# A decoder layer on one core: plain fp32 products for the experts and the router, and the experts' SiLU from one activation

## The reference

```python
scores = softmax(xt @ gate_w.T)
top_vals, top_idx = lax.top_k(scores, 2)
combine = sum(one_hot(top_idx, 8) * top_vals[..., None], axis=1)
h = silu(xt @ W1 + B1) * (xt @ W3 + B3)          # for each expert
acc = acc + c[:, None] * (h @ W2 + B2)
z = silu(xt @ sw1 + sb1) * (xt @ sw3 + sb3) @ sw2 + sb2   # the shared one
```

## Time and profile before

| | us |
|---|---|
| median of three executions | 1228.98 (1221.31 to 1236.30) |
| span of the profiled execution, first to last instruction | 1224.7 |
| PE / PEld busy | 929.7 / 700.9 |
| DVE busy | 922.6 |
| ACT busy | 489.6 |
| POOL busy | 528.2 |

### The profile page before, as it was taken

One profiled execution on the slowest core, in us unless ns is written; L12 is line 12 of the kernel. 1 busy time (PEld: TensorE's weight loads), 2 busy tenths in 40 slices (PEclk: granted clock), 3 DMA queues, 4 the chain that ended last, 5 costly groups with the idle time before them and its releaser, 6 DMA issues.

```text
span 1224.7 us, 13783 instructions
## 1 busy us (share of the span) xinstructions
PE 929.7 (76%) x3960; PEld 700.9 (57%) x3960; DVE 922.6 (75%) x1323; ACT 489.6 (40%) x911; POOL 528.2 (43%) x311
## 2 busy tenths in 40 slices
PE   4845549668689899577689899486789896677996
PEld 2434435256468685165477785165468683554885
DVE  2699996589999966689999965789789965322233
ACT  3534423544246434454345424454245421211442
POOL 1266540453457740533367730544257741001553
PEclk9855558778669999678679899678579997665999
DMA  5100101201023211101023211201023212000331
GB/s 193 36 35 35 52 1 35 70 35 61 18 70 121 77 45 54 70 35 61 18 78 127 73 36 55 85 18 61 18 72 119 86 35 91 21 1 9 117 109 42
DMA packets 38254, 72.61 MB, mean 59 GB/s; under 512 B 3871, under 2 KB 12712, under 8 KB 38174
## 3 DMA queue, kind: packets, MB, share of 16 engines
q1 hardware_dynamic: 38174, 71.65, 17.8%
HBM read 65.14 MB, written 2.30 MB: 55 GB/s over the span
## 4 chain that ended last, share of the span: by engine, by line
PE 45%; DVE 23%; issue 20%; POOL 6%; ACT 3%; DVEq 1%; POOLq 0%; DMA 0%; ACTq 0%; SPq 0%
PE ps L862 11%; DVE hs L1051 7%; PE ps L939 7%; PE ps L718 6%; PE ps L797 5%; POOL dbu L531 4%; DVE yacc L1103 4%; PE ps L836 3%; PE ps L791 2%; PE ps L825 2%; DVE work L1219 2%; PE ps L881 2%; PE ps L776 2%; DVE xn L1014 1%; POOL work L563 1%
## 5 line engine op out<-in xcount | busy, mean ns | idle before, releaser
L531 POOL TENSOR_TENSOR dbu<-v,bbc 128x1024 f32<-128x1024 f32 x128 | 308.9, 2418 | 257.3 <-DVE hs L1051 136.3
L1051 DVE TENSOR_TENSOR_SCAN hs<-ps,carry,dbu 128x512 f32<-128x512 f32 x256 | 313.3, 1266 | 10.1 <-ACT ps L627 8.2
L627 ACT ACTIVATE ps<-delta,neg_a 128x512 f32<-128x512 f32 x256 | 175.7, 692 | 300.5 <-DVE hs L1051 300.4
L718 PE MATMUL ps<-ident,hs 128*128 128x128 f32 x1024 | 189.1, 344 | 116.5 <-DVE yacc L1103 99.5
L718 PEld LDWEIGHTS ps<-ident,hs 128*128 128x128 f32 x1024 | 157.0, 180 | 150.0 <-DVE hs L1051 72.4
L1103 DVE SCALAR_TENSOR_TENSOR yacc<-ps,ctok,yacc 128x512 f32<-128x512 f32 x240 | 167.3, 737 | 1.2 <-PE ps L718 1.0
L555 POOL TENSOR_TENSOR w_lo<-w13s,w_hi 128x512 fp32r<-128x512 f32 x72 | 94.5, 1313 | 145.1 <-ACT w_hi L693 145.1
L939 PE MATMUL ps<-w2s,work 128*128 128x256 f32 x576 | 140.4, 388 | 0.3
L939 PEld LDWEIGHTS ps<-w2s,work 128*128 128x128 f32 x576 | 109.0, 196 | 15.9 <-DVE work L1225 1.5
L1219 DVE SCALAR_TENSOR_TENSOR work<-work 128x512 f32<-128x512 f32 x72 | 82.3, 1143 | 46.5 <-POOL work L563 45.6
L862 PE MATMUL ps<-x_hi,w_hi 128*128 128x512 f32 x288 | 107.9, 457 | 9.4 <-DVE work L1225 9.2
(11 more groups left out here) (159 smaller groups left out, 1243.0 us busy)
## 6 DMA issues: line engine op xcount, KB each, us to landing
w13s<-in_w SPq DMA_DIRECT2D x72, 256.0 KB, 2.9
bbc<-brow_dram SPq DMA_DIRECT2D x32, 512.0 KB, 4.0
w2s<-in_w SPq DMA_DIRECT2D x36, 256.0 KB, 2.7
cbc<-comb_dram SPq DMA_DIRECT2D x32, 256.0 KB, 3.5
work<-work SPq DMA_DIRECT2D x16, 256.0 KB, 2.3
xn<-in_x SPq DMA_DIRECT2D x5, 512.0 KB, 5.3
xt<-in_x SPq DMA_DIRECT2D x4, 512.0 KB, 3.6
rope<-in_rope_q SPq DMA_DIRECT2D x4, 512.0 KB, 4.2
```

The lines of the kernel that those rows point to most:

```text
L531: pool.tensor_tensor(dbu[:, i % DRING, :, :], v[:, 2 * h:2 * h + 2, :], bbc[:, n // 2 % 2, n % 2, :].rearrange("p (o t) -> p o t", o=1) .t ...
L627: act.activation(ps[:, unit % 2, :], delta[:, q, :], ACT.Exp, scale=neg_a[:, q * NS + m:q * NS + m + 1]).then_inc(da_done.sem, 1)
L718: last = pe.transpose(ps[:, bank, t * P:(t + 1) * P], src(t), ident[:, :])
L1051: dve.tensor_tensor_scan(hs[:, m % 2, q, 0:TC], ps[:, unit % 2, :], dbu[:, n % DRING, q % 2, :], carry[:, m, q:q + 1], ALU.mult, ALU.add). ...
```

## The change

The gate products and the router's scores are formed in plain fp32 from the arrays as they are. The fp32r parts w13_hi, w13_lo, x2_hi, x2_lo and wgate_parts, and the instructions that write them, are gone; x2t, a plain copy of the transposed input, shares x1t's place. Each gate product is 2 plain products instead of 6 fp32r instructions. ScalarE writes SiLU(a + b1) with one activation, Silu; th and gm are gone, and VectorE writes hh from ga or gac at once. The ring w13s has 5 places instead of 3, and `load_half` waits for the W3 product that last read the place.

```diff
-HRING = 3
+HRING = 5
...
-        x2_hi = sb("x2_hi", [P, KD, TC])
-        x2_lo = sb("x2_lo", [P, KD, TC])
+        x2t = x1t
...
             def load_half(j, c):
-                if c >= HRING:
-                    sp.wait_ge(*lo_done.at(j, c - HRING + 1))
-                else:
-                    sp.wait_ge(*lo_done.at(j, 0))
+                sp.wait_ge(*b_ps.at(j, max(0, c - HRING + 1)))
...
-                c = t - T_EXP + 1 + HRING
+                c = t - T_EXP - 1 + HRING
                 if HRING <= c < 2 * ALL:
                     load_half(j, c)
...
-                    c = t - T_EXP + 1
-                    if 0 <= c < 2 * ALL:
-                        pool.wait_ge(*hi_done.at(j, c + 1))
-                        pool.tensor_tensor(w13_lo[:, c % HRING, :, :, :].bitcast(F32R), w13s[:, c % HRING, :, :, :],
-                                           w13_hi[:, c % HRING, :, :, :], ALU.subtract).then_inc(lo_done.sem, 1)
                     c = t - T_EXP - 1
                     if 2 <= c < 2 * ALL:
...
-                        pool.wait_ge(*gm_done.at(j, c - 1))
+                        pool.wait_ge(*hh_done.at(j, c - 1))
...
-                        act.activation(x2_hi[:, k, :].bitcast(F32R), ps[:, 4 + k, :], ACT.Copy).then_inc(x2hi_done.sem, 1)
-                c = t - T_EXP + 1
-                if 0 <= c < 2 * ALL:
-                    act.wait_ge(*w13_in[c % HRING].at(j, 16 * (c // HRING + 1)))
-                    act.wait_ge(*b_ps.at(j, max(0, c - HRING + 1)))
-                    act.activation(w13_hi[:, c % HRING, :, :, :].bitcast(F32R), w13s[:, c % HRING, :, :, :], ACT.Copy
-                                   ).then_inc(hi_done.sem, 1)
+                        act.activation(x2t[:, k, :], ps[:, 4 + k, :], ACT.Copy).then_inc(x2t_done.sem, 1)
...
                     act.wait_ge(*a_ps.at(j, c + 1))
-                    act.wait_ge(*gm_done.at(j, max(0, c - 1)))
-                    act.activation(ga[:, ib, :], ps[:, 4, :], ACT.Identity, scale=0.5, bias=bias
-                                   ).then_inc(ga_done.sem, 1)
-                    act.activation(th[:, ib, :], ps[:, 4, :], ACT.Tanh, scale=0.5, bias=bias
-                                   ).then_inc(th_done.sem, 1)
+                    act.wait_ge(*hh_done.at(j, max(0, c - 1)))
+                    act.activation(ga[:, ib, :], ps[:, 4, :], ACT.Silu, bias=col("b1", c)).then_inc(ga_done.sem, 1)
...
-                    pe.wait_ge(*lo_done.at(j, c + 1))
-                    pe.wait_ge(*th_done.at(j, c))
+                    pe.wait_ge(*w13_in[c % HRING].at(j, 16 * (c // HRING + 1)))
+                    pe.wait_ge(*ga_done.at(j, c))
                     gate_rows(j, c, 0, a_ps)
...
             def gate_rows(j, c, s, sig):
-                products(ps[:, 4 + s, :], lambda w, k: w[:, c % HRING, s, k, :], (w13_hi, w13_lo),
-                         lambda x, k: x[:, k, :], (x2_hi, x2_lo)).then_inc(sig.sem, 1)
...
+                for k in range(KD):
+                    last = pe.matmul(ps[:, 4 + s, :], w13s[:, c % HRING, s, k, :], x2t[:, k, :],
+                                     start=(k == 0), stop=(k == KD - 1))
+                last.then_inc(sig.sem, 1)
...
-                    pe.wait_ge(*x2lo_done.at(j, KD))
+                    pe.wait_ge(*x2t_done.at(j, KD))
                     for tile in range(NT):
...
+                        for k in range(KD):
+                            last = pe.matmul(ps[:, 6, tile * EXPERTS:(tile + 1) * EXPERTS],
+                                             x2t[:, k, tile * P:(tile + 1) * P], wgate[:, k, :],
+                                             start=(k == 0), stop=(k == KD - 1))
...
-                    dve.wait_ge(w_att.sem, 5 * 16)
-                    dve.tensor_copy(wgate_parts[:, :, 0:EXPERTS].bitcast(F32R), wgate[:, :, :]).then_inc(gate_split.sem, 1)
...
-                if t == T_GATE:
-                    for k in range(KD):
-                        dve.wait_ge(*x2hi_done.at(j, k + 1))
-                        dve.tensor_tensor(x2_lo[:, k, :].bitcast(F32R), ps[:, 4 + k, :], x2_hi[:, k, :], ALU.subtract
-                                          ).then_inc(x2lo_done.sem, 1)
...
-                    dve.wait_ge(*th_done.at(j, c + 1))
                     if c < 2:
                         dve.wait_ge(*ga_done.at(j, c + 1))
                     else:
                         dve.wait_ge(*gac_done.at(j, c - 1))
-                    dve.wait_ge(*hh_done.at(j, max(0, c - 1)))
-                    dve.scalar_tensor_tensor(out=gm[:, ib, :], in0=th[:, ib, :], scalar=1.0,
-                                             in1=(gac if c >= 2 else ga)[:, ib, :],
-                                             op0=ALU.add, op1=ALU.mult).then_inc(gm_done.sem, 1)
-                    dve.wait_ge(*gm_done.at(j, c + 1))
                     dve.wait_ge(*b_ps.at(j, c + 1))
                     dve.wait_ge(*o_ps.at(j, max(0, c - 1)))
                     dve.scalar_tensor_tensor(out=hh[:, ib, :], in0=ps[:, 5, :], scalar=col("b3", c),
-                                             in1=gm[:, ib, :], op0=ALU.add, op1=ALU.mult).then_inc(hh_done.sem, 1)
+                                             in1=(gac if c >= 2 else ga)[:, ib, :], op0=ALU.add, op1=ALU.mult
+                                             ).then_inc(hh_done.sem, 1)
...
-                dve.tensor_copy(lg_low[:, :, :], sums[:, :, 1, :]).then_inc(lg_low_done.sem, 1)
-                dve.wait_ge(*lg_low_done.at(j, 1))
-                dve.tensor_tensor(lg[:, :, :], sums[:, :, 0, :], lg_low[:, :, :], ALU.add).then_inc(lg_done.sem, 1)
+                dve.tensor_copy(lg[:, :, :], ps[:, 6, 0:NT * EXPERTS].rearrange("p (t e) -> p t e", t=NT)
+                                ).then_inc(lg_done.sem, 1)
```

44 lines of the change are left out of this document (5 added, 39 removed).

## The result

The changed kernel takes 1253.18 us (median of four executions, 1241.24 to 1257.10) against 1231.60 us for the kernel before on the same chip: ratio 1.0178, 95% interval 1.0105 to 1.0252. In a second comparison it took 1247.32 us, ratio 1.0149 (1.0084 to 1.0214). It is slower, by 1.5 to 1.8%. The forecast was 1255 us with 1237 to 1292, so the total came out as forecast. Its composition did not, and part of the agreement is luck; that is what the rest is about.

The account below looks back on a forecast made before the run. TensorE was taken to bound most steps, VectorE steps 6 to 10. Overlapped walks +13.3, last walk +13.4 and start -0.35 gave +26.4 us on the 1224.7 span, 1251.1; forecast median 1255 us, range 1237 to 1273.

Parts of the forecast that it names:

- TensorE's steps: Expert steps: plain gate products cost 0.5 to 0.7 us more per tick; 6.06 us beside a scan, 5.17 in last walk.
- Steps 6 to 10: VectorE's slow stretch in overlapped walks: losing four gm makes TensorE the bound, 30.47 to 25.3 us, -5.2 (-6.2 to 0).
- Table loads: ScalarE: 81 to 87 more loads of 1.28 us, each behind its wait, covered by TensorE's 6.06 us in overlapped ticks.
- +1.3 at each loop head: Head of each of three overlapped walks: the input's copy may get its own table load, 0 to 1.30 us, 1.30 taken.
- +1.3 for the attention's Exp: Last walk: the attention's Exp needs a table load, +1.3 us.
- +1.4 for the last walk's first Silu: Last walk: the first Silu needs a table load and step 1 waits for ga, +1.4 us.
- first rival: Overlapped ticks: table loads bind ScalarE; at 2.6 us a load, +45 us gives 1300 us; chance 0.16.
- third rival: ScalarE: one table serves both Silu and Exp, no load alternates, only 4 to 7 us go, 1249 us; chance 0.05.
- Steps 0 to 2: Router and first steps of an overlapped walk: earlier router start against first products at the low clock, together +0.3 us.
- second rival: Steps 0 to 2 of each walk: TensorE's 2.4 GHz clock granted two products earlier, 20 us in all, 1235 us; chance 0.10.
- Sum of the overlapped walks: Three overlapped walks: +7.7 - 5.2 + 0.3 + 0.35 + 1.3 = +4.4 us each, +13.3 in all.
- the forecast's own +4.3: Whole run: the median time lies 4.3 us above the span of the trace, added to get from span to forecast.

Follow-up runs that it names:

- eighth run: The changed kernel with four of the eight instructions of each gate product, summing only half of the rows; 1153.32 us in one execution.
- second run: The kernel before with split products kept, but SiLU as one Silu activation and no gm; 1217.08 us, ratio 0.9914 to the kernel before.
- first run: The changed kernel with plain products but the old SiLU back (ga, tanh and VectorE's gm); 1243.53 us, ratio 1.0127 to the kernel before.
- third run: The changed kernel with Tanh in Silu's place, so that no table load alternates; 1247.93 us, ratio 1.0154 to the kernel before.
- eleventh run: The changed kernel with the scaling of xn as one VectorE instruction instead of four; 1241.58 us, ratio 1.0079 to the kernel before.
- ninth run: Split products, Silu table and one-instruction scaling of xn, plus a fourth term (low by low) in each gate product; 1245.43 us, ratio 1.0118 to the kernel before.
- seventh run: The changed kernel with forty extra TensorE transposes ahead of the feed-forward product; 1243.28 us, ratio 1.0131 to the kernel before.
- fifth run: The kernel before with the one Silu activation, no gm, and the scaling of xn in one instruction, products split; 1189.81 us, ratio 0.9732.

## Why the prediction was right, and where it was not

**TensorE's steps: right.** 6.04 and 5.16 us against 6.06 and 5.17 forecast; the price of a plain instruction read off the attention's product, 0.429 us, is that of the gate product. The eighth run confirms that 4 of them are 1.72 us. Last walk: 15 x 0.68 = 10.2 us against 10.4.

**Steps 6 to 10: right in kind, for the wrong reason.** They gave back 6.3, 8.6 and 6.5 us, where 5.2 was taken (with -6.2 as the end of its range). The step that failed is that in the slow stretch it is gm whose removal counts. Without gm the stretch is 1.4 us shorter in the first walk (second run, 29.12 for 30.47), with the plain products and gm still in place 6.3 (first run, 24.14). Single instructions of VectorE got shorter: over the run gm takes 1143 ns on average in the kernel before and 825 in the first run.

```profile
L1174 DVE SCALAR_TENSOR_TENSOR work<-work 128x512 f32<-128x512 f32 x72 | 59.4, 825 | 1.9 <-ACT work L685 1.9
```

What differs between them is GpSimd's remainder, 94.5 us of work, and ScalarE's copy. The trace of the kernel before speaks for GpSimd: 36 of its 72 gm have no GpSimd work beside them, and these take 0.66 to 0.69 us; two of the four in the slow stretch, with GpSimd at work beside them for 2.3 and 2.9 us, take four times as long:

```profile
393.67 2.85 DVE L1219 SCALAR_TENSOR_TENSOR work<-work 128x512 f32<-128x512 f32 x1 [0.33 <-POOL work L563]
400.98 2.86 DVE L1219 SCALAR_TENSOR_TENSOR work<-work 128x512 f32<-128x512 f32 x1
```

That the remainder alone is the cause was not isolated: no run took it away and left the rest.

**Table loads: the conclusion right, the step wrong.** 86 more loads, as forecast. The claim that a load stands behind the wait and can't be hidden, read off the row at 30.79, is wrong for these: Silu's load runs ahead of the wait, in idle time; in the changed kernel each of the 43 starts 0.02 us behind the activation before it. So the terms +1.3 at each loop head, +1.3 for the attention's Exp and +1.4 for the last walk's first Silu were not there; together 6.6 us too much. The third run prices all loads at nothing. The first rival (1300 us) fails on both grounds: the loads have cover, and where they have none (eighth run) a switch costs 1.30 us. The Trainium skill, page "ScalarE: Activation LUTs", section "What ACT_TABLE_LOAD costs", puts a drain of 1380 ns beside the load; its 1283 ns for the load agree with the trace, and the drain appears in no run here, with 4.61 us for a cycle of two switches. The third rival, one table for both functions, fails with the 86 loads.

**Steps 0 to 2:** forecast +0.3, measured -0.9, +0.1 and -1.3 us from the first SiLU to the third. Most of this gain is only a later start: the product of step 0 takes 0.86 us more, the first SiLU comes that much later, and the step behind it ends with the wait for the weights, which hides the product as forecast. From the transposes of the router's input to the third SiLU the three walks differ by -0.5, +0.5 and -0.9 us. The second rival fails here: the product of step 0 still runs at the low clock in every walk (3.76 us for its four instructions).

**Sum of the overlapped walks.** Forecast +4.4 each, 13.3 in all. Measured -1.2 in the experts' steps and -5.7 between two of the walks and the next scan, in part again the clock: the kernel before has 7 to 11 us at the low level in that stretch, the changed one 3.4 to 3.9.

**The attention stages: not forecast at all.** The prediction priced the clock only around the router, and its second rival had it come earlier. Instead the three stages are 20.2 us longer. Of these 7.3 us are the change's own, above all the normalisation that GpSimd's second product slows; the prediction priced nothing for the removal of GpSimd's remainder there, and it costs 2.0 us a stage. The other 12.9 us are the clock. Without them the span would be about 1237 us, 12 us or 1.0% above the kernel before, and the median by the forecast's own +4.3 about 1241.5 us (an estimate): within the range, but 13 us below the 1255. The change was priced 14 us too high and the clock 13 us too low; that the two cancelled is luck.

Which stages the clock makes long is open. Kernels with plain products and one activation had the second and third stage long, 120.5 to 122.5 us, in all five traces, the half products included; those with split products had them between 109.8 and 115.3 in all five traces of theirs with tanh or three terms, and at 110.6 with four; the first run had one of each. Counted over all three stages, the feed-forward product ran at the low clock, some 5 us longer, in 12 of 15 stages of those five traces, in 3 of 18 of the split ones (all three with tanh), in one of three of the first run and in none of the eleventh. Yet the eleventh run, plain and with Silu, has both at 114. So, as far as the runs go, the long stages come neither from the plain form alone, nor (in one trace) from how full TensorE is in the walk ahead of them (ninth run), nor from the table loads (third run), and more TensorE work that ends 13 us ahead of the product does not mend them (seventh run). What decides when the clock is granted stays open, and so does whether the long stages are the kernel's or chance between executions: ten long stages of ten in five traces speak for the first, the eleventh run, whose edit moves VectorE by 0.15 us in each walk and by some 2 us in each of the two scalings ahead of them, for the second.

Without the attention's clock, the change is worth about +10.7 us for the last walk, +7.3 for the attention stages, and -1 to -7 for the rest of the overlapped walks. Even with short stages it is not faster: the trace of the eleventh run, with all three short, spans 1227.0 us, those of the kernel before, with one long feed-forward product each, 1224.7 and 1224.8. The run as a whole has the ratio 1.0079, and the fastest of its ten executions took 1227.56 us against 1220.76 for the kernel before beside it.

## What to carry to other kernels

Price a change of TensorE's instructions by a row of the same form and clock; here that held to 0.02 us a step. Before a removed instruction is called free, look at what the other engines' instructions cost beside it: the same VectorE instruction took 0.34 to 2.42 us depending on what ran with it. A removed instruction can also cost: without GpSimd's remainder its next product ran beside VectorE's normalisation, 2.0 us more in each attention stage. And test the two halves of a change apart: the plain products cost time, the Silu table alone gained 0.9%, and with the scaling in one instruction the kernel is at 0.9732 of the time before.

## What the runs showed of the hardware that was not expected

- ScalarE's table load for an activation that waits on a semaphore runs ahead of that wait when the instruction before it is done (427.76 against 430.47 us); 86 more of them lengthened no walk.
- Four TENSOR_SCALAR of 128x256 on VectorE lasted 1.37 us with GpSimd idle, 3.27 us with 2.15 us of GpSimd's work beside them and 5.30 us with 4.55. One lasted 0.34 us at the least and 2.42 us at the most, and the longest are as long as one dbu product on GpSimd (2.4 us). The slowing goes both ways: 2.25 us for a GpSimd instruction of 1.28.
- The scans and the sums on VectorE (means 1266 and 737 ns before, 1265 and 736 after and in the fifth run) are not slowed by GpSimd's work: in the kernel before a scan takes 1.25 to 1.28 us, both the 98 with none of it beside them and the 118 with it all through.
- The granted clock of a stage can differ between two traces whose kernels differ in one VectorE operation of another stage: 0.50 and 0.68 over the same 79 TensorE instructions, 33.70 and 28.73 us. A higher mean over the run (0.826 against 0.801) did not bring the long stages down. And TensorE worked for 12.45 us without a gap at the low level in one trace (601.20 to 613.65), where the same instructions after the same idle times had the high one within 1 us in another.
